# Two packed weight arrays, four transfers each, and the first x_t issued behind the feed-forward weights

## What is computed

```python
# attention layer; the conditioning weight is chosen per batch
c = einsum('bsi,boi->bso', x, weight[cond_id])            # 512x512, one of 8
q, k, v = c @ Wq, c @ Wk, c @ Wv                          # 32 heads, 8 key/value groups, head size 16
q, k = rope(q), rope(k)
x = x + softmax(causal(q k^T) / 4) v @ Wo
# feed-forward layer; the LoRA factor is chosen per batch
y = x @ W.T + 0.5 * (x @ lora_A[lora_id]) @ lora_B.T      # rank 32
base = y @ W_base.T + b_base
top 2 of 8 experts by y @ W_router.T, softmaxed
x = x + base + 2 * sum over experts of gate * (y @ A_e.T) @ B_e   # rank 16 each
```

## Time and profile before

| | us |
|---|---|
| median of 3 runs | 237.53 |
| lowest, highest | 237.14, 239.57 |
| the profiled execution, own time | 237.22 |
| its span, first to last instruction | 235.4 |

### The profile page before, as it was taken

How to read it: one execution, slowest core, us unless ns; L and a number is a source line. 1 busy time by engine, 2 the same in 40 slices (tenths; PEclk the granted TensorE clock), 3 DMA queues, 4 the chain that set the end, 5 groups by cost and what they waited for, 6 DMA issues and landing times.

```text
span 235.4 us, 5807 instructions
## 1 busy us (share of the span) xinstructions
PE 221.1 (94%) x2010; PEld 173.7 (74%) x2010; DVE 172.3 (73%) x905; ACT 117.2 (50%) x287; POOL 96.2 (41%) x110
## 2 busy tenths in 40 slices
PE   6699997998999999999999999999999999899893
PEld 6588885786778876877687778777876776477693
DVE  0599838947864997589757975898489849948873
ACT  3697442686586257526752675266622650171210
POOL 7020570857369074707480748064922320002020
PEclk9999999999999999999999999999999999999999
DMA  4999508007002602260116011601101010003011
GB/s 131 319 387 361 202 1 277 6 0 226 3 3 56 225 3 58 55 213 4 57 52 218 4 56 47 223 3 57 45 3 47 13 45 3 0 4 102 0 47 45
DMA packets 20050, 21.18 MB, mean 90 GB/s; under 512 B 6453, under 2 KB 11573, under 8 KB 20021
## 3 DMA queue, kind: packets, MB, share of 16 engines
q1 hardware_dynamic: 20020, 20.81, 27.4%
HBM read 18.71 MB, written 2.10 MB: 88 GB/s over the span
## 4 chain that ended last, share of the span: by engine, by line
PE 77%; DVE 12%; ACT 4%; issue 2%; DMA 2%; SPq 1%; DVEq 0%; ACTq 0%
PE bank L1125 14%; PE bank L1126 12%; PE bank L1130 12%; PE bank L1152 5%; PE bank L1216 4%; PE bank L1178 4%; PE bank L1231 3%; PE bank L1136 3%; DVE thrown L794 3%; PE bank L1233 2%; PE bank L1232 2%; DMA stage_d<-base_t 2%; PE bank L1310 2%; ACT late L472 2%; DVE qkv_w_lo L724 2%
## 5 line engine op out<-in xcount | busy, mean ns | idle before, releaser
L373 POOL TENSOR_TENSOR cond_w_lo<-cond_raw,cond_w_hi 128x512 fp32r<-128x512 f32 x28 | 35.5, 1291 | 48.1 <-ACT cond_w_hi L472 48.1
L794 DVE CUSTOM_DVE_ANT_0 thrown<-bank,causal 128x64 f32<-128x64 f32 (+1 forms) x256 | 47.3, 253 | 0.6 <-issue 0.5
L393 POOL TENSOR_TENSOR rope_b<-rope_a,rope_b 128x128 f32<-128x128 f32 (+1 forms) x16 | 16.1, 1021 | 25.9 <-DVE rope_b L850 25.9
L472 ACT ACTIVATE max_rows<-bank,own_p 128x128 fp32r<-128x128 f32 x32 | 9.2, 369 | 33.3 <-PE bank L1162 33.3
L402 POOL TENSOR_TENSOR x_bias<-x,bias_row 128x512 f32<-128x512 f32 x8 | 10.3, 1290 | 28.7 <-DVE out_sb L974 27.3
L1125 PE MATMUL bank<-qkv_w_hi,c_t_hi 128*128 128x256 f32 (+1 forms) x64 | 21.4, 352 | 0.4 <-DVE c_t_lo L724 0.3
L1125 PE MATMUL bank<-fused_w_hi,late 128*128 128x324 f32 (+2 forms) x68 | 20.6, 318 | 0.9 <-ACT late L472 0.2
L794 DVE DVE_READ_ACCUMULATOR2_ANT neg_max<- 128x1 f32 x256 | 21.3, 83 | 0.0
L1126 PE MATMUL bank<-qkv_w_lo,c_t_hi 128*128 128x256 f32 (+1 forms) x64 | 20.3, 338 | 0.0
L1126 PE MATMUL bank<-fused_w_lo,late 128*128 128x324 f32 (+2 forms) x68 | 19.7, 306 | 0.0
L472 ACT ACTIVATE cond_w_hi<-cond_raw 128x512 fp32r<-128x512 f32 x32 | 17.5, 622 | 1.0 <-DMA cond_raw<-cond_w_t 1.0
(11 more groups left out here) (166 smaller groups left out, 631.4 us busy)
## 6 DMA issues: line engine op xcount, KB each, us to landing
cond_raw<-cond_w_t SPq DMA_DIRECT2D x7, 1024.0 KB, 5.5
xt_raw<-x_t SPq DMA_DIRECT2D x8, 256.0 KB, 5.9
x_nat<-x SPq DMA_DIRECT2D x8, 256.0 KB, 2.6
out<-out_sb SPq DMA_DIRECT2D x8, 256.0 KB, 2.0
stage_d<-base_t SPq DMA_DIRECT2D x4, 256.0 KB, 4.8
cond_raw<-cond_w_t SPq DMA_DIRECT2D x4, 256.0 KB, 4.6
stage_b<-w SPq DMA_DIRECT2D x4, 256.0 KB, 5.5
stage_a<-w_q SPq DMA_DIRECT2D x4, 256.0 KB, 5.9
```

Of the source, the lines that this page charges most:

```text
L373: pool.tensor_tensor(cond_w.lo[:, k, :], cond_raw[:, k, :], f32(cond_w.hi[:, k, :]), ALU.subtract).then_inc(cond_lo, 1)
L393: pool.tensor_tensor(qk[:, at:at + w], rope_a[:, at:at + w], rope_b[:, at:at + w], ALU.add).then_inc(qk_ready, 1)
L472: return nc.scalar.activation(out, in_, ACT.Copy, scale=scale)
L794: nc.vector.tensor_tensor_reduce(thrown[:, b % 2, j, e, 0:width // 2] .rearrange("p (a s) -> p a s", a=h + 1), scores[:, :, e, :], causal[ ...
```

## The change

The router, the experts' A and the base weight are laid side by side by the host as one array `ffn_t` of 512 rows by 648 columns, and loaded in four transfers of 128 rows (2,592 bytes a row, 324 KB) instead of six transfers. q and k|v become one array `w_qkv` of 512 rows by 768 columns, loaded in four transfers (3,072 bytes a row, 384 KB) instead of eight. x_t of batch 0 is issued behind lora_b and the feed-forward weights; it was the first transfer behind the ids. The order of all compute instructions is the same.

```diff
-                sp.dma_start(xt_raw[:, :, :], x_t[0:1, :, :]...).then_inc(xt_in, 16)
                 sp.dma_start(lora_b_raw[:, :, :], lora_b.rearrange("(k p) r -> p k r", p=P)).then_inc(lb_in, 16)
-                for src, at in ((router_t, 0), (experts_a_t, EXPERTS)):
-                    sp.dma_start(stage_ffn[:, :, at:at + src.shape[1]], src.rearrange("(k p) n -> p k n", p=P)
-                                 ).then_inc(ffn_in, 16)
-                for k in range(KT):
-                    sp.dma_start(stage_ffn[:, k, GATES:FFN], base_t[k * P:(k + 1) * P, :]).then_inc(base_in[k], 16)
+                for k in range(KT):
+                    sp.dma_start(stage_ffn[:, k, :], ffn_t[k * P:(k + 1) * P, :]).then_inc(ffn_in[k], 16)
+                sp.dma_start(xt_raw[:, :, :], x_t[0:1, :, :]...).then_inc(xt_in, 16)
                 sp.wait_ge(ids_in, 32)
...
                 for k in range(KT):
-                    sp.dma_start(stage_qkv[:, k, D:QKV], w_kv[k * P:(k + 1) * P, :]).then_inc(qkv_in[k], 16)
-                    sp.dma_start(stage_qkv[:, k, 0:D], w_q[k * P:(k + 1) * P, :]).then_inc(qkv_in[k], 16)
+                    sp.dma_start(stage_qkv[:, k, :], w_qkv[k * P:(k + 1) * P, :]).then_inc(qkv_in[k], 16)
...
             def split_qkv(k):
-                act.wait_ge(qkv_in[k], 32)
+                act.wait_ge(qkv_in[k], 16)
...
             def split_ffn(k):
-                act.wait_ge(ffn_in, 32)
-                act.wait_ge(base_in[k], 16)
+                act.wait_ge(ffn_in[k], 16)
```

More of the change, by code:

```diff
@@ L17, with build_program @@
 MASKED = -3.0e38
-def build_program(nc, x, x_t, cond_ids, lora_ids, cond_w_t, w_q, w_kv, w_o, cos, sin, w2, lora_a, lora_b,
-                  base_t, base_bias, router_t, experts_a_t, experts_b, out):
+def build_program(nc, x, x_t, cond_ids, lora_ids, cond_w_t, w_qkv, w_o, cos, sin, w2, lora_a, lora_b, ffn_t, base_bias,
+                  experts_b, out):
     BATCH, T, D = x.shape
@@ L33, in build_program @@
     HD = cos.shape[1]
-    KV = w_kv.shape[1] // 2
+    KV = (w_qkv.shape[1] - D) // 2
     GROUPS = KV // HD
@@ L40, in build_program @@
     assert KV == P and TILE == 32 and PAIRS == 4 and PER == 4
-    EXPERTS = router_t.shape[1]
-    RANK = experts_a_t.shape[1] // EXPERTS
+    EXPERTS = ffn_t.shape[1] - D - experts_b.shape[0]
+    RANK = experts_b.shape[0] // EXPERTS
     LR = lora_a.shape[2]
@@ L185, in build_program @@
         w2_in = [sem(f"w2_in{k}") for k in range(KT)]
-        base_in = [sem(f"base_in{k}") for k in range(KT)]
-        o_in, ffn_in, b_in, lb_in = sem("o_in"), sem("ffn_in"), sem("b_in"), sem("lb_in")
+        ffn_in = [sem(f"ffn_in{k}") for k in range(KT)]
+        o_in, b_in, lb_in = sem("o_in"), sem("b_in"), sem("lb_in")
         out_free = sem("out_free")
@@ L287, in first_loads @@
                 sp.dma_start(ids[0:1, BATCH:2 * BATCH], lora_ids.rearrange("(a n) -> a n", a=1)).then_inc(ids_in, 16)
+                sp.dma_start(lora_b_raw[:, :, :], lora_b.rearrange("(k p) r -> p k r", p=P)).then_inc(lb_in, 16)
+                for k in range(KT):
+                    sp.dma_start(stage_ffn[:, k, :], ffn_t[k * P:(k + 1) * P, :]).then_inc(ffn_in[k], 16)
                 sp.dma_start(xt_raw[:, :, :], x_t[0:1, :, :].rearrange("a (k p) s -> p (a k) s", p=P)
                              ).then_inc(xt_in, 16)
-                sp.dma_start(lora_b_raw[:, :, :], lora_b.rearrange("(k p) r -> p k r", p=P)).then_inc(lb_in, 16)
-                for src, at in ((router_t, 0), (experts_a_t, EXPERTS)):
-                    sp.dma_start(stage_ffn[:, :, at:at + src.shape[1]], src.rearrange("(k p) n -> p k n", p=P)
-                                 ).then_inc(ffn_in, 16)
-                for k in range(KT):
-                    sp.dma_start(stage_ffn[:, k, GATES:FFN], base_t[k * P:(k + 1) * P, :]).then_inc(base_in[k], 16)
                 sp.wait_ge(ids_in, 32)
@@ L1580 @@
         "cond_w_t": lay(a["L0_cond_weight"].transpose(0, 2, 1)),
-        "w_q": lay(a["L0_attn_Wq"].reshape(D, GROUPS, PER, HD).transpose(0, 2, 1, 3).reshape(D, D)),
-        "w_kv": lay(np.concatenate([a["L0_attn_Wk"], a["L0_attn_Wv"]], axis=1)),
+        "w_qkv": lay(np.concatenate([a["L0_attn_Wq"].reshape(D, GROUPS, PER, HD).transpose(0, 2, 1, 3).reshape(D, D),
+                                     a["L0_attn_Wk"], a["L0_attn_Wv"]], axis=1)),
         "w_o": lay(a["L0_attn_Wo"].reshape(GROUPS, PER, HD, D).transpose(1, 0, 2, 3).reshape(D, D)),
@@ L1588 @@
         "lora_b": lay(a["L0_cond2_lora_B_w"]),
-        "base_t": lay(a["L0_ffn_W_base"].T),
+        "ffn_t": lay(np.concatenate([a["L0_ffn_W_router"].T, a["L0_ffn_A"].reshape(experts * rank, D).T,
+                                     a["L0_ffn_W_base"].T], axis=1)),
         "base_bias": lay(a["L0_ffn_b_base"]),
-        "router_t": lay(a["L0_ffn_W_router"].T),
-        "experts_a_t": lay(a["L0_ffn_A"].reshape(experts * rank, D).T),
         "experts_b": lay(a["L0_ffn_B"].transpose(0, 2, 1).reshape(experts * rank, D)),
```

## The result

| | before | changed |
|---|---|---|
| median | 237.53 us | 236.25 us |
| lowest, highest | 236.84, 239.57 | 235.70, 237.65 |
| the profiled execution | 237.22 us, span 235.4 | 235.77 us, span 234.0 |

The ratio is 0.9947, with a 95% interval of 0.9926 to 0.9967: 1.3 us by the medians, 0.9 was forecast (236.6). The changed kernel was run once more beside the later experiments: 236.37 against 237.37, 1.0 us, ratio 0.9974 (0.9951 to 0.9997). The two intervals overlap from 0.9951 to 0.9967, a gain of 0.8 to 1.2 us, and the forecast lies there.

What follows compares the result with a forecast made beforehand. The start, up to the first k|v product at 23.84 us, was taken as bound by the weight stream. Small pieces -0.64 and lora_g slack -0.26 gave -0.90 us, 236.6 against the median 237.53; range 235.2 to 237.9 us.

Steps and rivals of the forecast that it cites:

- What bounds: Before 24 us, a stream of bytes with DVE and PE close behind; the change acts only on the first k|v product.
- Issues: nothing: On SP, fewer issues send the 6.48 us tile out at about 5.4, worth nothing since the DMA queue is 2 us deep.
- Small pieces: 0.64 us: At the stream's start, packing recovers 0.64 of the 1.39 us that short pieces of x_t, A, lora_b and router lose.
- What I kept in for lora_b and x_t (0.23 and 0.20): Loss in the early stream that stays: lora_b still in 128-byte pieces costs 0.23 us, x_t in 512-byte pieces 0.20.
- The dip of 0.83 us: Slow stretch of the stream at 6 to 7.75 us, losing 0.83 us; likeliest it stays, wherever the stream then is.
- The rival that the small pieces alone cause the dip: The 6 to 7.75 us slow stretch is the small pieces' backlog and goes too: 235.2 to 235.9 us, chance 0.20.
- Long rows, q and k|v: nothing: In the stream, 2,592-byte rows cost what 2 KB rows do, and joining q with k|v gains nothing: 0 us each.
- The 4%: Feed-forward rows not beginning on 256-byte boundaries would lose 4% of 3.4 us, estimated 0.15 us, by the skill's page.
- x_t: covered: x_t behind the feed-forward weights lands at 9.35 us, 1.5 us before ACT used it, so costs 0.
- The tie at lora_g, +0.26: DVE's 2 us lead shrinks at lora_g, behind ACT's copy after the second w2 tile, to 0.64 + 0.26 = 0.90 us.
- POOL against DVE: POOL's x_t low part slows one feed-forward low part on DVE by 0.97 us; this stays, or goes into lora_g's wait.
- Sum: Whole kernel: small pieces -0.64, slack at lora_g -0.26, all else 0, together -0.90 us, to 236.6 us; likeliest case 0.55.

Runs made afterwards that it cites:

- two more issues: Changed kernel with two 32-byte transfers into a spare tile on SP ahead of the first conditioning tile: 236.63 us, ratio 0.9968; 236.59 us at full clock.
- long pieces: Changed kernel with x_t and lora_b laid out by partition on the host, 2 KB and 512 bytes in a piece: 235.95 us, ratio 0.9957.
- the run with w2 first: Changed kernel with the four w2 tiles issued ahead of lora_b and the feed-forward weights: one execution, 239.11 us.
- The order alone: Kernel before with x_t alone moved behind the base weight and nothing packed: 237.63 us, ratio 1.0019.
- the filled one: Changed kernel with x_t and lora_b in longer pieces, two ACT copies earlier, and eight idle matmuls on PE at 37 to 40 us: 235.98 us, ratio 0.9944.
- padded rows: Changed kernel with feed-forward rows 2,816 bytes apart, of which 2,592 are read, so each begins on a 256-byte boundary: 236.4 us, ratio 0.9956.
- SP later: Changed kernel with one more read of an id into a register on SP ahead of the first conditioning tile: 236.55 us, ratio 0.9972.

## Why the prediction was right

**What bounds.** Right. The rest of the program took 211.4 us for 211.6, and the gain is made ahead of the first k|v product.

**Issues: nothing.** Not borne out. The tile that went out at 6.48 went out at 5.32, as forecast (5.4), but at full clock 0.57 us of SP's time cost 0.5 us, and two more issues 0.56. "The queue in front of the engines is 2 us deep" was too sure: their share was 0.65 and 0.61 from 4 to 5 us of the kernel before, and with two more tiny transfers it fell to 0.90 in 9 to 12.5 us. By the estimate above this term may be most of the gain; it is not settled.

**Small pieces: 0.64 us.** The stream gained more, and not by the pieces alone. Up to 12 us 0.80 were recovered by the same measure, and at the second w2 tile 14.29 - 13.29 = 1.0 us, in which SP's earlier issues are contained. The run with as many issues as before, at full clock, leaves 237.04 - 236.59 = 0.45 us (237.04 is the kernel before in the same measurement) for the pieces and for the 0.4 us by which its first conditioning tile is still earlier than before. What I kept in for lora_b and x_t (0.23 and 0.20) did not come back with long pieces (0.1 us for both). For x_t the rate was misread: 297 GB/s is that of 3.0 to 3.5 us, where the stream has just begun, and not of 512-byte pieces as such. From 5 to 6 us of the kernel before, 382 of 485 packets are under 2 KB, 51 of them under 512 bytes, and the rate is 381 GB/s. The dip of 0.83 us was treated as something that stays in place or goes; it did neither. The slow beginning and the dip of before, 1.08 + 0.31 + 0.83 = 2.22 us, became 0.91 + 0.53 + 0.11 = 1.55: in this profile the stream has one slow stretch, at 4.50 to 6.00, where before the short pieces and the dip each took their own. The rival that the small pieces alone cause the dip fell by the run with w2 first, where a slow stretch came without any ahead of it.

**Long rows, q and k|v: nothing.** Right, by one run each, for q and k|v within 0.2 us. The 4% that the forecast worked out from the Trainium skill ("DMA: Bandwidth & Descriptors", How a descriptor splits into AXI transactions) did not show: 390 GB/s for these rows. The spacing of the feed-forward tiles was forecast as 0.85 us; in the changed kernel it was 1.65, 0.90 and 0.89.

**x_t: covered.** Right: expected to land at 9.35, it landed at 9.23 and its copy started at 9.26, 1.6 us before that of before. The order alone gave 1.0019. Its use is that DVE has its idle time in front of lora_g instead of in front of the feed-forward parts.

**The tie at lora_g, +0.26.** Right in place and size: DVE stood idle there 0.69 us, and the lead of 1.0 us of the stream became 1.21 at DVE. Moving ACT's copies brought the product forward by 0.75 us, and the time by 0.4.

**POOL against DVE.** The two met again, at less: the four conditioning parts took 3.03 us, for 3.46, since POOL (9.97 to 11.26) had begun in DVE's idle time. It went into the wait for lora_g, as said.

**Sum.** 0.90 us forecast, 1.21 at the product, 1.4 in the span, 1.0 and 1.3 by the medians, 1.1 at full clock. What bounds, the place of the tie and the total are right. The split is not: the gain was put on the small pieces and nothing on SP's time, and the runs give SP's time a large part. That the total came out so near is in part luck.

## What to carry to other kernels

Where the start of a kernel is a stream of weights, add up the bytes ahead of the tile that the compute chain really waits for and ask at what rate they move; packing short arrays into long ones gave 1.1 us of 237 here, and reordering x_t gave nothing. Do not take the issues for free because the DMA engines look full: half a microsecond of SP's time ahead of the conditioning tiles cost half a microsecond. To learn how much is the pieces and how much the issues, change one without the other. Then look for in-order places where an engine that is ahead has to stand behind a tile of the stream for work that doesn't need it: moving two copies ahead of such a tile gave 0.4 us at full clock, over a third of what the whole change gave. And compare kernels whose clock falls in some executions by the executions at full clock: a median or a ratio also counts how often it fell.

## What the runs showed that was not expected

- The head of the stream has a slow stretch whether w2 or the feed-forward array comes first: 1.3 us between the second and third of four 256 KB tiles where the pace is 0.67, and the fourth feed-forward tile at 8.1 to 8.7 us in nine of ten profiles with the changed kernel's order, though the tiles before it land differently. In the changed kernel the DMA engines' share is 0.90 and 0.94 meanwhile, so they are busy and move less; why is not shown.
- PE's granted clock fell from 1.00 to 0.50, from its level of 2.4 to that of 1.2 GHz, for some 3.4 us behind a stretch of three microseconds in which PE was busy for 0.31, 0.51 and 0.71, in some executions and not in others: the changed kernel's profile shows 0.59, 0.65 and 0.35 there and a clock of 1.00 behind it. Four profiles of kernels with several executions had such a drop; from the product on they took 213.0 to 213.4 us, those of the other kernels 211.4 to 212.1, and that is the distance of the two groups of times. The Trainium skill ("TensorE: Matmul & The Clock Gate", What's actually happening) has the clock follow how busy PE has been. The traces agree in so far as the clock fell behind a thin stretch, and was 1.00 behind the filled one (1.00, 0.98, 0.94). But how thin it was doesn't tell the outcome here: PE was busy for 1.59 us of 37 to 40 us in the changed kernel's profile, which kept its clock, and for 1.61 and 1.60 in the profiles with padded rows and with SP later, which had 0.55 and 0.53 in 40.5 to 43.8. What decides between them is not shown.
